# Attention with projected heads on one core: a semaphore for each weight tile, a new order of the first and last work, and the halves of v swapped

## The reference

```python
x = normal((16, 512, 32, 32)); w_proj = normal((1536, 512)); w_out = normal((512, 512))

def normalize_weight(w, eps=1e-4):                    # rows of 512
    n = norm(w, axis=1, keepdims=True)
    return w / (eps + sqrt(1 / 512) * n)

def pixnorm(x, eps=1e-8):
    return x / sqrt(mean(x * x, axis=-1, keepdims=True) + eps)

wp = normalize_weight(w_proj) / sqrt(512)
wo = normalize_weight(w_out) / sqrt(512)
h = einsum('oc,bcn->bno', wp, x.reshape(16, 512, 1024))
q, k, v = split(h.reshape(16, 1024, 8, 3 * 64), 3, axis=-1)
q, k, v = pixnorm(q) / 64 ** 0.25, pixnorm(k) / 64 ** 0.25, pixnorm(v)
attn = softmax(einsum('bihd,bjhd->bijh', q, k), axis=2)
res = einsum('bijh,bjhd->bihd', attn, v).reshape(16, 1024, 512)
res = einsum('oc,bnc->bon', wo, res)
return (0.7 * x + 0.3 * res) / sqrt(0.7 ** 2 + 0.3 ** 2)
```

## Time and profile before

| | before |
|---|---|
| median of three runs | 2988.52 us |
| profiled execution | 2986.36 us |
| its span | 2984.6 us |
| PE, busy | 2933.4 us, 98% |
| PEld, busy | 2013.6 us, 67% |
| DVE, busy | 2581.7 us, 87% |
| ACT, busy | 2383.4 us, 80% |
| POOL, busy | 454.9 us, 15% |
| mean granted TensorE clock | 0.999 |

### The profile page before, as it was taken

How to read it: one execution, slowest core, us unless ns; L and a number is a source line. 1 busy time by engine, 2 the same in 40 slices (tenths; PEclk the granted TensorE clock), 3 DMA queues, 4 the chain that set the end, 5 groups by cost and what they waited for, 6 DMA issues and landing times.

```text
span 2984.6 us, 85445 instructions
## 1 busy us (share of the span) xinstructions
PE 2933.4 (98%) x36928; PEld 2013.6 (67%) x36928; DVE 2581.7 (87%) x3197; ACT 2383.4 (80%) x2993; POOL 454.9 (15%) x678
## 2 busy tenths in 40 slices
PE   7999999999999999999999999999999999999998
PEld 5776666766667667676666766667666666666765
DVE  6898888988889888898888988888888888988887
ACT  6887878878778778787787877878787787878786
POOL 0210121101211112112111111012110121101210
PEclk9999999999999999999999999999999999999999
DMA  3133414333242332333323333223323334334234
GB/s 106 41 56 63 91 36 108 51 79 79 44 97 50 81 78 48 90 62 76 72 52 85 62 79 69 65 72 62 85 63 69 76 54 96 60 63 86 40 80 103
DMA packets 459529, 211.04 MB, mean 71 GB/s; under 512 B 407952, under 2 KB 407952, under 8 KB 459152
## 3 DMA queue, kind: packets, MB, share of 16 engines
q1 hardware_dynamic: 459152, 205.58, 32.3%
HBM read 71.30 MB, written 33.55 MB: 35 GB/s over the span
## 4 chain that ended last, share of the span: by engine, by line
PE 79%; DVE 8%; POOL 5%; ACT 3%; DMA 3%; issue 2%; SPq 0%; ACTq 0%; DVEq 0%
PE ps_pv L973 21%; PE ps_score L952 19%; PE ps_dense L930 11%; PE ps_dense L932 10%; PE ps_dense L934 10%; DVE probs L780 4%; PE ps_dense L989 3%; PE ps_dense L990 2%; PE ps_dense L991 2%; DMA x_raw<-in_x 2%; POOL rs_t L442 1%; POOL rs_t L444 1%; POOL rs_t L446 1%; ACT e_tile L596 1%; DVE probs L771 1%
## 5 line engine op out<-in xcount | busy, mean ns | idle before, releaser
L780 DVE TENSOR_TENSOR probs<-e_tile,probs 128x1024 f16<-128x1024 f32 x1024 | 1241.4, 1230 | 64.6 <-ACT probs L603 58.7
L596 ACT ACTIVATE e_tile<-ps_score,shift 128x1024 f32<-128x1024 f32 x1024 | 1107.9, 1118 | 223.7 <-PE ps_score L952 130.2
L973 PEld LDWEIGHTS ps_pv<-v_pair,probs 128*128 128x128 f16 x24576 | 772.2, 98 | 183.5 <-issue 112.4
L973 PE MATMUL ps_pv<-v_pair,probs 128*128 128x65 f16 (+1 forms) x24576 | 821.6, 193 | 2.9 <-DVE probs L780 1.7
L952 PE MATMUL ps_score<-qkT 64*128 64x512 f16 x6144 | 753.4, 378 | 3.3 <-ACT e_tile L596 3.1
L930 PE MATMUL ps_dense<-wpT_hi,x_hi 128*128 128x512 f32 x1536 | 621.0, 404 | 2.4 <-DVE wpT_lo L851 2.3
L932 PE MATMUL ps_dense<-wpT_lo,x_hi 128*128 128x512 f32 x1536 | 600.1, 391 | 0.0
L934 PE MATMUL ps_dense<-wpT_hi,x_lo 128*128 128x512 f32 x1536 | 599.0, 390 | 0.0
L603 ACT ACTIVATE probs<-e_tile 128x1024 f16<-128x1024 f32 x512 | 542.8, 1061 | 22.8 <-PE ps_pv L973 4.0
L952 PEld LDWEIGHTS ps_score<-qkT 64*128 64x128 f16 x6144 | 257.0, 94 | 361.4 <-issue 90.2
L771 DVE CAST probs<-e_tile 128x1024 f16<-128x1024 f32 x512 | 360.0, 703 | 72.0 <-PE ps_pv L973 67.6
...
## 6 DMA issues: line engine op xcount, KB each, us to landing
x_raw<-in_x SPq DMA_DIRECT2D x128, 256.0 KB, 3.4
x_res<-in_x SPq DMA_DIRECT2D x128, 256.0 KB, 3.6
out<-x_res SPq DMA_DIRECT2D x128, 256.0 KB, 2.5
arena<-in_w_proj SPq DMA_DIRECT2D x24, 128.0 KB, 2.9
qkT<-arena SPq DMA_TRANSPOSE x128, 4.8
resT<-res_split SPq DMA_TRANSPOSE x128, 3.6
...
```

The costliest lines, as they stand in the source:

```text
L596: act.activation(e_tile[:, t % E_BUFS, :, :], ps_score[:, t % 2, :, :], ACT.Exp, bias=shift[:, 0:1], scale=1.0 / (QK_UP * QK_UP)).then_inc ...
L780: dve.tensor_tensor(probs_of(b, t, 1), e_tile[:, t % E_BUFS, :, :], probs_of(b, t, 0), ALU.subtract).then_inc(probs_low, 1)
L973: mm = pe.matmul(ps_pv[:, h, o:o + n], probs_of(b, t, part)[:, h, queries], v[:, cols], start=(j == 0 and it == 0 and part == 0 and cols.s ...
```

## The change

Four things in one diff:
- `w_loaded` becomes one semaphore for each tile of w_proj (two DMAs each) and one for w_out, thirteen in place of four. `load_weights(m)` loads one tile, and `square_weights(m)` waits for its own tile.
- The table FIRST is replaced, on all engines. SyncE's order of the first loads was: tiles 0 to 3, x 0 and 1, tiles 4 to 7, x 2 and 3, tiles 8 to 11, x 4 and 5, w_out, x 6 and 7. It becomes: x 0, tiles 0 to 5, x 1, tile 6, x 2 and 3, tiles 7 to 9, x 4, tiles 10 and 11, w_out, x 5 to 7. VectorE begins x_lo 0, norm chain 0, x_lo 1, w_scale 0 to 2, x_lo 2, w_scale 3, w_low 0 to 2, x_lo 3, w_low 3 (before: norm chain 0, x_lo 0, w_scale 0, x_lo 1, w_scale 1 and 2, w_low 0, w_scale 3, w_low 1 and 2, x_lo 2 and 3, w_low 3). ScalarE begins x_hi 0, squares 0 to 4, x_hi 1, squares 5 and 6, x_hi 2. TensorE's order changes between transpose 5 and attend 4.
- The table LAST is replaced. Pieces 0 and 1 of batch 15 are loaded in batch 13. At the end the order on TensorE is attend 29, out 0, out 1, attends 30 and 31, out 2 (before: attend 29, out 0, attends 30 and 31, out 1), on VectorE low_p 61, add 0, low_p 62 and 63, add 1, take 7 (before: low_p 61 to 63, add 0, take 7, low_res 7, add 1), on ScalarE finish 0 and 1, high_res 7 (before: high_res 7, finish 0 and 1), on SyncE turn_res 5, stores 14.6 and 14.7, turn_res 6, load_res 0 and 1, store 0, load_res 2, store 1, load_res 3, turn_res 7.
- In `v_pair` the low part moves from element 72 to 0, and the high part with the ones from 0 to 64.

STEADY is not changed. The core of the diff:

```diff
 FIRST = {
-    "LOAD_X_AT": (12256, 12272, 12304, 12320, 12352, 12368, 12400, 12416),
+    "LOAD_X_AT": (12096, 12208, 12240, 12256, 12320, 12384, 12400, 12416),
-    "W_LOAD_AT": (12240, 12288, 12336, 12384),
+    "W_LOAD_AT": (12112, 12128, 12144, 12160, 12176, 12192, 12224, 12272, 12288, 12304, 12336, 12352, 12368),
...
 LAST = {
-    "LOAD_X_AT": (-76992, -44054, -43915, -43560, -43544, -43464, -12848, -11632),
+    "LOAD_X_AT": (-77376, -70888, -43560, -43547, -43542, -43504, -13152, -12544),
...
         SUMS = D + 1
-        LOW = D + 8
+        HIGH = D
         VCOLS = 2 * D + 32
         v_pair = sb("v_pair", [P, 4, NT, VCOLS], F16)
...
-        w_loaded = [sem(f"w_loaded{g}") for g in range(W_GROUPS)]
+        w_loaded = [sem(f"w_loaded{m}") for m in range(WP_TILES + 1)]
...
-            def load_weights(g):
-
-                if 4 * g >= WP_TILES:
-                    sp.dma_start(w_raw[:, 4 * g:4 * g + 4, :], wo_in).then_inc(w_loaded[g], 16)
+            def load_weights(m):
+
+                if m == WP_TILES:
+                    sp.dma_start(w_raw[:, WP_TILES:, :], wo_in).then_inc(w_loaded[m], 16)
                     return
-                for i in range(GROUP_UNITS):
-                    p, kind = LAYOUT[GROUP_UNITS * g + i]
-                    for h in range(2):
-                        sp.dma_start(w_raw[h * D:(h + 1) * D, 4 * g + i, :],
-                                     wp_in[2 * p + h, WEIGHT_ROWS[kind], :, :]).then_inc(w_loaded[g], 16)
+                p, kind = LAYOUT[m]
+                for h in range(2):
+                    sp.dma_start(w_raw[h * D:(h + 1) * D, m, :],
+                                 wp_in[2 * p + h, WEIGHT_ROWS[kind], :, :]).then_inc(w_loaded[m], 16)
...
             def square_weights(m):
-                act.wait_ge(w_loaded[m // 4], 16 * (8 if m < WP_TILES else 1))
+                act.wait_ge(w_loaded[min(m, WP_TILES)], 16 * (2 if m < WP_TILES else 1))
...
-                dve.tensor_tensor(v[:, :, :, LOW:LOW + D],
+                dve.tensor_tensor(v[:, :, :, 0:D],
                                   proj[:, ring(g, half), at_col:at_col + 2 * D]
                                   .rearrange("p n (h d) -> p n h d", d=D),
-                                  v[:, :, :, 0:D], ALU.subtract).then_inc(v_low, 1)
+                                  v[:, :, :, HIGH:HIGH + D], ALU.subtract).then_inc(v_low, 1)
...
-                            for part, cols in ((0, slice(0, SUMS)), (0, slice(LOW, LOW + D)), (1, slice(0, SUMS))):
+                            high, low = slice(HIGH, HIGH + SUMS), slice(0, D)
+                            for part, cols in ((0, high), (0, low), (1, high)):
```

More of the change, by code:

```diff
@@ L528, in task @@
             def task(b, s, when):
-                for g in when["w_load"].get(s, ()):
-                    load_weights(g)
+                for m in when["w_load"].get(s, ()):
+                    load_weights(m)
                 for piece in when["load_x"].get(s, ()):
@@ L574, in high_v @@
                 heads = slice(2 * (p % 2), 2 * (p % 2) + 2)
-                act.activation(v_pair[:, heads, half * HALF_NT:(half + 1) * HALF_NT, 0:D]
+                act.activation(v_pair[:, heads, half * HALF_NT:(half + 1) * HALF_NT, HIGH:HIGH + D]
                                .rearrange("p h n d -> p n h d"),
```

140 lines of the change are left out of this document (70 added, 70 removed), and 30 rows, old and new, of tables (FIRST, LAST).

## The result

The changed kernel takes **2999.21 us** (median of 7 runs, 2996.26 to 2999.8) beside 2988.01 us for the kernel before (7 runs, 2987.12 to 2990.43): ratio 1.0033, 95% interval [1.0022, 1.0043]. It is 11 us slower, where 5 us less were forecast; the time lies 12 us over the top of the forecast's own range (2987) and 10 over the wider one (2989). Its profiled execution took 2999.77 us, its span is 2998.0 us, 13.4 over the span before.

What follows compares the result with a forecast made beforehand. TensorE was taken as the bound nearly everywhere, VectorE at the last batch's end. Start -3.3, x of the last batch -1.9, end +0.4 and swap 0 summed to -4.8, giving 2983.7 us; own range 2981 to 2987, wider 2974 to 2989.

Steps and rivals of the forecast that it cites:

- The start: First batch: early x piece and squares as tiles land start the first projection at 19.1 us, 3.6 us earlier.
- For these I take 0.3 back: First batch: late tile 7 (2.2 us of cover), tight piece 7 and last w_low cost 0.3, leaving -3.3 for the start.
- The clock: Shortly after TensorE's start: same half-speed stretch as before, 1.9 us lost; none would give -1.9, a second +1.9.
- That wait goes: -1.9: Batch 14: earlier loads of x end ScalarE's 3.45 us wait and TensorE's 1.57 us wait, -1.9 us.
- Together the end is +0.4: End of the last batch: +0.6 + 1.3 - 2.2 + 0.7 us, with ends -2.5 and +3.5.
- The small terms: Last batch: VectorE's extra low_res +0.6, its norm wait and order +1.3, out 0's transposes +0.7, out 4 +0.2 us.
- from there the loads of x_res no longer trail: Last outputs: with loads of x_res no longer waited for, the last add comes 2.2 us sooner, -2.2.
- The swap: Halves of v_pair exchanged, judged on the attention matmuls: 0 taken, at most 13 us either way.
- rival (d): Swap of v_pair slows attention matmuls reading from element 64: at 1 ns each +11 us, 2995; chance 7%.
- Rival (c): Swap of v_pair removes half of the attention matmuls' 25 us over the rate: 2971 us; chance 12%.
- The order is untouched and the same stall stays: Batches 1 to 13: the stall on the x load stays as before, with no term in the sum.
- (a): Start's gain not carried or eaten by the end, as late pieces, slow clock or transpose 6: +1, 2989.5 us; chance 14%.

Runs made afterwards that it cites:

- e4_sems: Kernel before with thirteen weight semaphores and squares as tiles land, loads in their old order: 2986.74 us, ratio 0.9993.
- e6_first_fix: Kernel before with thirteen semaphores and the new FIRST, but w_out loaded behind x piece 5 and scale 4 behind low_p 7: 2988.40 us.
- e9_change_x: The whole changed kernel, plus x piece 5 of the next batch loaded ahead of store 5 in batches 0 to 13: 2976.37 us.
- e3_last: Kernel before with the new table LAST alone: 2997.39 us, ratio 1.0028.
- e12_last_x: e7_xload with the new table LAST, nothing else: 2972.71 us.
- e5_last_fix: Kernel before with the new LAST, but x_hi and x_lo of piece 6 behind exp 35 and the last stores and loads in pairs: 2994.15 us.
- e8_xload_swap: e7_xload with the halves of v_pair swapped as in the change, nothing else: 2968.63 us.
- e7_xload: Kernel before with x piece 5 of the next batch loaded ahead of store 5 in batches 0 to 13: 2966.96 us.
- e1 to e6: Six kernels, each the kernel before with one part of the change (swap, FIRST, LAST or semaphores), two with places put back: 2986.74 to 2997.39 us.

## Why the prediction failed, point by point

**The start: the mechanism right, the tenth luck.** Table load 3.83 (forecast 4.1), norm chain 9.07 (9.7), w_scale 0 12.99 (13.5), w_scale 4 21.87 (22.4), first projection 19.11 (19.1). The steps are 0.3 to 0.6 us early, and the way from w_scale 0 to the first projection is 0.5 us longer than forecast, which cancels; the other traces with this order have up to 20.55. And I gave the gain to both, order and semaphores; e4_sems shows 2.95 of the 3.6 us with the old order.

**"For these I take 0.3 back": wrong, it was all of it and more.** I costed the cover of tile 7 and of piece 7 and missed two others. First, I let piece 5 land as any piece does and named w_out without counting its 1 MB ahead of it on the same queue: 7.5 us instead of 3.4. With w_out behind it (e6_first_fix) the same piece took 4.4. The Trainium skill (DMA: Bandwidth & Descriptors, "Queues, rings and completion order") says that each DMA engine takes the descriptors of one queue in their order; the trace agrees, since w_out, issued 0.6 us earlier on the same queue, lands 0.6 us earlier (27.68 and 28.32). By the Trainium skill's fabric ceiling (DMA: Bandwidth & Descriptors, Specifications), an estimate, 1 MB takes 2.4 us, so the piece would land after 5.8; the trace has 7.5, and 7.4 for w_out itself.
Second, I read VectorE's new order only up to w_low 3 and asked only what is late at the start. Scale 4 ahead of low_p 7 put a wait for GpSimd in front of work that TensorE needed: 1.9 us, in three traces. The norm itself is slower there, 8.6 us from its first instruction to its last (80.85 to 89.44) against 7.6 before (86.76 to 94.31). GpSimd, the changed kernel:

```profile
83.23 1.15 POOL L446 TENSOR_TENSOR rs_t<-rs_t,shift 128x64 f32<-128x64 f32 x1
...
86.82 0.29 POOL L446 TENSOR_TENSOR rs_t<-rs_t,shift 128x64 f32<-128x64 f32 x1
```

The same instruction takes 1.15 us beside a low_p of VectorE (82.94 to 84.23) and 0.29 us while VectorE idles. The Trainium skill (GPSIMD Engine Reference, 1. Specifications) says that GpSimd shares its SBUF interfaces with VectorE, with contention when a VectorE instruction has two inputs in SBUF, as low_p has; the trace agrees.

**The clock.** I took one half-speed stretch, 1.9 us, as before. There it is: 0.05 x 22.7 + 0.02 x 37.3 = 1.9. The second one that I had put into the bounds (+1.9) came too: 0.02 x 70 = 1.4 in 60 to 130. It follows the idle time of attends 3 in the changed kernel, but not the same idle time in e9_change_x; what decides that is open.

**"That wait goes: -1.9": the step that failed.** The stall of the earlier trace rows at 2534.66 is not in batch 14. Attends of batch 13 run there, and the load is of x for batch 14, which STEADY orders. I had named the batch by the x, and the diff's table by the batch that runs. The place that LAST does order is 2700 to 2730, where x of batch 15 is split, and there TensorE had no idle time to give back. The new order made one: +2.0 us. The timeline of that stretch before, on record in the same trace, would have shown it.

**"Together the end is +0.4": +5.3 came (from attend 16 of batch 14 on: 0.9 + 1.1 + 0.2 + 3.1), and the largest term has the wrong sign.** The small terms held: +1.9 for VectorE's order and its wait for the norm (that wait is 1.45 us at 2898.45, 0.8 more than before, forecast 1.3 more) against +1.1 up to attend 28 of batch 15, 0.7 for out 0 against a wait of 0.5 us at 2963.74, and +0.2 for out 4 against +0.3 (2977.74 less 2967.35 less the 10.1 by which attend 28 was late). Two things failed. The order of batch 14's end was not costed at all, and a full VectorE that got its work in another order cost +0.9 there. And "from there the loads of x_res no longer trail", -2.2, was +3.1. I priced a store at 2.1 us until its load goes, from two stores issued together, and the load at 3. In the new order each store runs beside the other buffer's load, and the four stores ahead of a load took 2.3, 3.2, 4.85 and 3.4 us (to 2978.27, 2981.81, 2987.49, 2991.23). The 4.85 is there again at the same store in e3_last, e9_change_x and e12_last_x (4.7 to 4.8). In pairs (e5_last_fix) they took 2.1, 2.1, 3.3 and 2.3. That the mixing of stores and loads is what slows them was not tried by itself. A second, smaller part is SyncE's order: the store at 2987.86 stands behind the load that waits until 2987.49; its own data were ready at 2986.9 (add 2985.56, then finish), 1 us. My expectation of e5_last_fix took the order for the whole.

**The swap: 0 forecast, +1.7 measured** (e8_xload_swap less e7_xload). Inside my bounds, but not where I looked for it: I costed the attention matmuls, which did run at the old rate, and the 1.7 us lie in the projections behind them. It is rival (d)'s direction at a tenth of its 16 us. Rival (c), 12%, has nothing for it. Two slips in the recorded text: the two forms differ by one column (0.4 ns), not two, with which the 1.6 ns come out; and 16.4 less 4.8 is 11.6 us over the time before, 3000, not 2995. That the measured 2999 lies next to this is chance, since rival (d)'s mechanism is not there.

**Batches 1 to 13: not in the sum at all.** "The order is untouched and the same stall stays" was true, yet a stall on a load has no fixed size. In the 13 stalls of these batches ScalarE waits 40.8 us for x in the changed kernel and 38.5 before, 1.9 to 3.5 us each (another 4.2 of its 48.5 in all, against 44.0, are at the start). Of the 4.3 us that come there some 1.6 are the swap's; the rest is gone once the load is moved (e9_change_x). How much of that rest is the change's doing and how much one execution's stays open: from attend 8 of batch 0 to attend 12 of batch 14 the kernels e1 to e6, with that table untouched too, drift from -0.9 to +4.3 us (the changed kernel 4.2).

**The rivals.** (a) had the mechanism, each cover failing, but at +1 us for a start and an end that came to +9 (1.7 + 4.4 + 3.1); all chances of "slower" together were 0.09. I had built the range from what could fail in the steps that I had followed, and most of the loss lay in steps that I had not: piece 5, scale 4, x_hi 6 of batch 15, VectorE in batch 14, the stores at the end.
